# Batch 0's expert results from the result slots straight into the merge's buffer

## The reference

```
grouped = x.reshape(b, s // g, g, d)                       # groups of 32 tokens, 16 groups a batch
logits = einsum('bntd,des->bntes', grouped, Wc) + bc + tie
perm = (logits == max(logits, axis=-3))                    # every expert picks one token of each group
permuted = einsum('bntd,bntes->bnesd', grouped, perm)
inner = relu(einsum('bnesd,esdf->bnesf', permuted, W1) + b1)
result_permuted = einsum('bnesf,esdf->bnesd', inner, W2) + b2
result = einsum('bnesd,bntes->bntd', result_permuted, perm)
x = x + tanh(g_ffn[0]) * result
```

## Time and profile before

| | |
|---|---|
| median of 3 runs | 1321.31 us |
| lowest and highest | 1316.73 and 1325.94 us |
| profiled execution | 1322.05 us |
| its span, first to last instruction | 1320.3 us |
| mean granted TensorE clock | 0.986 |
| TensorE, VectorE, ScalarE, GpSimd busy | 1252.8, 887.4, 570.1, 552.6 us |
| DMA | 213.59 MB, mean 162 GB/s |

### The profile page before, as it was taken

One profiled execution on the slowest core, in us unless ns is written; L12 is line 12 of the kernel. 1 busy time (PEld: TensorE's weight loads), 2 busy tenths in 40 slices (PEclk: granted clock), 3 DMA queues, 4 the chain that ended last, 5 costly groups with the idle time before them and its releaser, 6 DMA issues.

```text
span 1320.3 us, 28354 instructions
## 1 busy us (share of the span) xinstructions
PE 1252.8 (95%) x10607; PEld 901.3 (68%) x10607; DVE 887.4 (67%) x1570; ACT 570.1 (43%) x1039; POOL 552.6 (42%) x456
## 2 busy tenths in 40 slices
PE   8999999999999978886999999999998999999998
PEld 7777677777777657621447666766775778887887
DVE  6985677777676455564547766766685977777762
ACT  4255245534442554453562443353336434333331
POOL 3303642553251100000339657866834644454540
PEclk9999999999999998998999999999998999999999
DMA  9885465234411678899993643563423111111100
GB/s 351 220 184 185 138 183 173 79 113 150 142 65 45 209 206 273 308 402 368 403 337 116 213 167 99 176 221 123 133 84 129 64 64 64 64 49 47 64 29 35
DMA packets 126502, 213.59 MB, mean 162 GB/s; under 512 B 27609, under 2 KB 49369, under 8 KB 122331
## 3 DMA queue, kind: packets, MB, share of 16 engines
q1 hardware_dynamic: 126427, 212.57, 48.7%
HBM read 129.92 MB, written 82.62 MB: 161 GB/s over the span
## 4 chain that ended last, share of the span: by engine, by line
PE 76%; DVE 9%; DMA 5%; SPq 3%; issue 3%; ACT 3%; POOL 1%; DVEq 0%; ACTq 0%; POOLq 0%
PE b L157 12%; PE b L158 11%; PE b L159 11%; PE b L1606 5%; PE b L1805 5%; PE b L1806 4%; PE b L1807 4%; PE b L1577 4%; PE b L1712 3%; PE b L1720 3%; PE b L2135 3%; PE b L2101 3%; PE b L1626 2%; PE b L2119 2%; SPq L709 2%
## 5 line engine op out<-in xcount | busy, mean ns | idle before, releaser
L1169 ACT ACTIVATE a_pr<-b 120x512 f32<-120x512 f32 x252 | 130.1, 604 | 89.3 <-PE b L1606 89.3
L1358 DVE TENSOR_REDUCE a_mx<-b 128x4 f32<-128x480 f32 x256 | 151.8, 649 | 14.6 <-PE b L1577 14.4
L1050 POOL TENSOR_TENSOR a_rp<-a_rp,a_b2s 128x512 f32<-128x512 f32 x96 | 120.4, 1291 | 26.6 <-DMA a_rp<-s_rp 26.6
L1089 POOL TENSOR_TENSOR a_atl<-a_pvs,a_ath 128x512 fp32r<-128x512 f32 x64 | 81.2, 1302 | 79.1 <-ACT a_ath L1213 79.1
L1805 PE MATMUL b<-a_woh,a_ath 128*128 128x512 f32 x256 | 104.9, 410 | 3.1 <-POOL a_atl L1089 3.1
L157 PE MATMUL b<-a_xth,a_wqh 128*128 128x512 f32 x256 | 104.2, 407 | 0.6 <-DVE a_xtl L1333 0.4
L1807 PE MATMUL b<-a_woh,a_atl 128*128 128x512 f32 x256 | 101.8, 398 | 0.0
L158 PE MATMUL b<-a_xtl,a_wqh 128*128 128x512 f32 x256 | 101.8, 398 | 0.0
L1806 PE MATMUL b<-a_wol,a_ath 128*128 128x512 f32 x256 | 101.8, 398 | 0.0
L159 PE MATMUL b<-a_xth,a_wql 128*128 128x512 f32 x256 | 101.7, 397 | 0.0
L1503 DVE SCALAR_TENSOR_TENSOR a_x<-b,a_gate,a_x 128x512 f32<-128x512 f32 (+1 forms) x64 | 47.7, 745 | 72.5 <-PE b L1807 72.5
(11 more groups left out here) (245 smaller groups left out, 3127.3 us busy)
## 6 DMA issues: line engine op xcount, KB each, us to landing
a_rp<-s_rp SPq DMA_DIRECT2D x128, 256.0 KB, 4.6
s_x<-a_x SPq DMA_DIRECT2D x16, 1024.0 KB, 4.3
s_rp<-e_chosen SPq DMA_DIRECT2D x16, 1024.0 KB, 8.0
s_rp<-e_xc SPq DMA_DIRECT2D x16, 1024.0 KB, 8.0
e_w<-in_w SPq DMA_DIRECT2D x56, 256.0 KB, 5.1
a_xr<-in_x_t SPq DMA_DIRECT2D x8, 1024.0 KB, 6.5
a_x<-in_x SPq DMA_DIRECT2D x8, 1024.0 KB, 10.5
s_xn<-a_xn SPq DMA_DIRECT2D x8, 1024.0 KB, 4.6
```

Source lines behind the costliest of these rows:

```text
L1050: pool.tensor_tensor(rp[:, t, a], rp[:, t, a], b2s[:, :], ALU.add).then_inc(rp_biased, 1)
L1169: act.activation(pr[:, h % RING, :], bank[k][0:S2, :], ACT.Exp, scale=SCALE)\
L1358: dve.tensor_reduce(mx[:, t, :, r], bank[k][:, 0:HJ * S2].rearrange("p (a s) -> p a s", a=HJ), AX.X, ALU.max).then_inc(free[k], 1)
```

## The change

For batch 0, the rows go from the slot in SBUF to the merge's buffer `rp` in SBUF at once, and not by way of DRAM. For every unit below 16 and each of its two halves c, four transfers (one for each expert) bring 16 slot partitions x 2 KB into the one partition of `rp` that belongs to the expert, 32 KB each, and one transfer stores the other 48 partitions of the half to DRAM. These are ten transfers a unit where there was one; units 16 to 31 are stored as before. All ten count on `out_st`, so the counts are worked out by `stored`. The sixteen loads of batch 0 and SyncE's wait ahead of them are gone, and TensorE waits for `half_written` itself before each of the four tiles of batch 0. So that an expert's 16 rows lie in the order of `rp`, (t a), the gathered tiles go to `gt` with a step of 4 in place of 4 side by side, and the loads of the other batches read (j t a). The buffer `rp` moves to the head of the memory of `gt` (its first 32 KB), `wqh` and `wql` behind it.

```diff
-        allot(early, "wqh wql xth xtl rp xn permb b2h b2l bo x qh ql pvs woh wol pr ath atl kbd kl mpick vals pick bc b2s mx "
+        allot(early, "rp wqh wql xth xtl xn permb b2h b2l bo x qh ql pvs woh wol pr ath atl kbd kl mpick vals pick bc b2s mx "
@@ load_experts
-        src = io["rp"][of].rearrange("u (c j a t) s d -> (u c) s j t a d", c=2, a=GT, t=NT)
+        src = io["rp"][of].rearrange("u (c j t a) s d -> (u c) s j t a d", c=2, a=GT, t=NT)
@@ load_behind
         if u == HALF_U:
-            front.half_written(sp)
-            for t in range(NT):
-                load_experts(sp, 0, t)
             load_query_weight(sp)
@@ add_experts_bias
-                pool.wait_ge(rp_in[t], 16 * GT * (j + 1))
+                pool.wait_ge(rp_in[t], 16 * GT * j)
@@ merge_tile
-                pe.wait_ge(rp_in[t], 16 * GT * (j + 1))
+                if i is None:
+                    front.half_written(pe)
+                else:
+                    pe.wait_ge(rp_in[t], 16 * GT * j)
@@ experts.sync
-            sp.dma_start(io["rp"][2 * u // EK][u % (EK // 2)], slot(u)).then_inc(out_st[u % RO], 16)
+            if u < EK // 2:
+                for c in range(2):
+                    at, own, e = c * NH, NG // B, 2 * EJ * u + EJ * c
+                    for j in range(EJ):
+                        sp.dma_start(behind[0].rp[e + j:e + j + 1].rearrange("s t a d -> s (t a) d"),
+                                     slot(u)[at:at + own, j, :]).then_inc(out_st[u % RO], 16)
+                    sp.dma_start(io["rp"][0][u][at + own:at + NH], slot(u)[at + own:at + NH]).then_inc(out_st[u % RO], 16)
+            else:
+                sp.dma_start(io["rp"][1][u - EK // 2], slot(u)).then_inc(out_st[u % RO], 16)
             behind[0].load(sp, u)
 
-    def half_written(sp):
+    def stored(n):
+
+        return 16 * (2 * (EJ + 1) * min(n, EK // 2 // RO) + max(n - EK // 2 // RO, 0))
+
+    def half_written(eng):
         for q in range(RO):
-            sp.wait_ge(out_st[q], 16 * (EK // 2 // RO))
+            eng.wait_ge(out_st[q], stored(EK // 2 // RO))
@@ gathered
-        ts = slice(TS * a, TS * (a + 1))
+        ts = slice(a, GS, 4)
@@ scalar and vector, results(p)
-                act.wait_ge(out_st[u % RO], 16 * (u // RO))
+                act.wait_ge(out_st[u % RO], stored(u // RO))
```

More of the change, by code:

```diff
@@ L86 @@
 Begun = namedtuple("Begun", "load_ahead gather emptied evict_act evict_dve on_act chosen")
-Behind = namedtuple("Behind", "load act dve pe")
+Behind = namedtuple("Behind", "load act dve pe rp")
 Front = namedtuple("Front", "cleared half_written written groups_read spare_banks banks")
@@ L1841, in attention @@
             Behind(load_behind, lambda act, k: scalar(act, k), lambda dve, k: vector(dve, k),
-                   lambda pe, k: tensor(pe, None, k))
+                   lambda pe, k: tensor(pe, None, k), rp)
     ahead = Ahead(load_weights, load_first, load_first_keys, load_second, load_output_weight, constants, first_norm, query_weights_high, query_weights_low,
@@ L1983, in sync @@
                     sp.wait_ge(g_free[b], n + 1)
-            sp.dma_start(io["rp"][2 * u // EK][u % (EK // 2)], slot(u)).then_inc(out_st[u % RO], 16)
+            if u < EK // 2:
[7 more added lines that the diff above has]
+                sp.dma_start(io["rp"][1][u - EK // 2], slot(u)).then_inc(out_st[u % RO], 16)
             behind[0].load(sp, u)
-    def half_written(sp):
+    def stored(n):
+        return 16 * (2 * (EJ + 1) * min(n, EK // 2 // RO) + max(n - EK // 2 // RO, 0))
+    def half_written(eng):
         for q in range(RO):
-            sp.wait_ge(out_st[q], 16 * (EK // 2 // RO))
+            eng.wait_ge(out_st[q], stored(EK // 2 // RO))
     def written(eng, q):
-        eng.wait_ge(out_st[q], 16 * (EK // RO))
+        eng.wait_ge(out_st[q], stored(EK // RO))
     def gathered(c, s, a):
         b, _ = use(SETS * c + s, a)
-        ts = slice(TS * a, TS * (a + 1))
+        ts = slice(a, GS, 4)
         dst = gt[:, :, s, :, ts] if turned(c) else gt[:, s, :, :, ts]
@@ L2050, in results @@
             if p % 2 == 0 and u >= RO:
-                dve.wait_ge(out_st[u % RO], 16 * (u // RO))
+                dve.wait_ge(out_st[u % RO], stored(u // RO))
             for q in range(2):
```

## The result

| | before | after |
|---|---|---|
| median (range) of 4 runs each | 1323.62 us (1316.73 to 1327.86) | 1432.76 us (1426.43 to 1435.18) |
| profiled execution, its span | 1322.05, 1320.3 us | 1426.43, 1424.6 us |
| granted clock, mean of the span | 0.986 | 0.948 |

The changed kernel takes 1.0808 times as long, 95% interval 1.0774 to 1.0842. The forecast was 1473 us with a range of 1345 to 1515: direction and range hold, the size is 40 us too large.

What follows compares the result with a forecast made beforehand. TensorE bounds most of the kernel, but the full DMA engines bound the expert results. Units 0 to 15 at 12.6 us with constants +158.6, unit 16's store +2.5, loads -10.0: +151 on 1322.05 gives 1473 us, range 1345 to 1515.

Steps and rivals of the forecast that it cites:

- Part 1: Expert results: batch 0's sixteen loads and the queue's wait ahead of them go, -10.0 us, at most 17.2.
- unit 16's store: Expert results: this store, ahead of the point where units 0 to 15 are done before, falls behind it: +2.5 us.
- Part 2: Expert results: a unit's eight 32 KB transfers into one partition go at one engine's 26.3 GB/s, 10.0 us a unit.
- The keys' ratio of 1.41: Last keys' load: 32-partition rows hold the engines 1.41 times as long per byte, taken as sign that narrow destinations are slow.
- Part 3: Expert results: a unit's two 48-row stores take 2.6 us, 1.9 at the low end; with the transfers 12.6 a unit.
- Part 4: SyncE's queue: ten issues a unit at 0.36 to 0.47 us, 3.6 to 4.7 us, hidden under 12.6 us of data.
- Rival C: Expert results: one partition takes the full rate and SyncE's issues bound: +12 us, 1334 us; chance 0.12.
- Part 5: Edits at nothing: TensorE's wait before the merge and the step-4 gathered evictions cost 0 us; evictions above 650 ns would refute it.
- The sum: Whole kernel: units 0 to 15 and constants +158.6, unit 16's store +2.5, loads -10.0, so +151 us to 1473 us.
- A: Expert results, main case: transfers and stores run serially, 12.6 us a unit: 1473 us, range 1432 to 1510; chance 0.68.
- B: Expert results: transfers into different partitions overlap; two at a time 7.6 us a unit, 1394 us, four 1353; chance 0.15.
- D: Expert results: direct transfers hide altogether, units keep 2.5 to 2.9 us: 1305 to 1312, say 1308 us; chance 0.05.

Runs made afterwards that it cites:

- e7: e1 without the two stores a unit, so the direct transfers alone (batches 1 to 3 load other data): 1375.14 us, a unit 6.5.
- e3: e1 with each direct transfer writing 2 KB into each of 16 partitions and not 32 KB into one: 1411.51 us, a unit 8.78.
- e12: e4 with each direct transfer into 16 partitions and not one: 1383.99 us.
- e6: e1 without the direct transfers, so the two 48-row stores a unit alone (batch 0's buffer filled by one 4 MB load): 1335.92 us.
- e2: The kernel before with only the step-4 evictions and the loads' order that goes with them: 1337.18 us, ratio 1.0078.
- e1: The changed kernel with gathered evictions writing four side by side again, rp in order (a t), and a later SyncE wait before loading x: 1416.93 us.
- e8: e4 and e5 together: one whole store and four direct transfers from SyncE, four from ScalarE: 1353.12 us, a unit 5.06.
- e10: e8 with each direct transfer into 16 partitions and not one: 1345.28 us, a unit 4.78.
- e5: e1 with the four direct transfers of the half c = 1 issued from ScalarE's queue, not SyncE's: 1378.17 us, a unit 6.65.
- e9: e7 (direct transfers alone) with each transfer into 16 partitions and not one: 1365.09 us, a unit 5.53.
- e11: e1 with a unit's eight direct transfers first and then both 48-row stores: 1411.48 us, a unit 8.91.
- e4: e1 with one whole store of 128 rows a unit in place of the two of 48: 1388.62 us, a unit 7.25.

## Why the prediction was right, and where it was not

**What bounds the kernel before**: read rightly. The units stood on the critical path; 101.7 us more for them became 104 us of the whole.

**Part 1** held: from the units' end to the kernel's end it is -10.7 us; the -10.0 of the loads and the +2.5 of unit 16's store make -7.5.

**Part 2** is the step that failed. It put the unit's pace at eight transfers of one partition, 10.0 us at one engine's 26.3 GB/s, with sixteen engines held behind it. The rate was not far off for such transfers alone (e7: 34 GB/s at first, some 56 later), but in the changed kernel all transfers together kept the engines at a share of 0.57, and a wider destination changes the kernel by next to nothing (e3, e12). The keys' ratio of 1.41 was a true sign of a real effect, which was then given the whole unit.

**Part 3**: 2.6 us for the two stores; e6 has 2.64 for them alone in its last eight units. The sum 10.0 + 2.6, one behind the other, fell with part 2.

**Part 4** is where the pace was. "Under 12.6 us of data this is hidden" hid what decides. The price was too low as well: 0.36 to 0.47 us an issue came from the shortest and the median ones in the earlier trace rows, issues that stand singly or in fours. A better row was at hand: the earlier trace rows has sixteen back to back in 10.66 us, 0.67 each, and with 16 x 10 x 0.67 us for the units C's sum is already 1382 us. Here they are 0.59 back to back, and the issue behind each store adds 1.2 us: 8.7 a unit and not 3.6 to 4.7. Rival C named the mechanism, the share "well below 1, SyncE's queue without gaps" word for word, and with these two prices its own sum, 558.84 + 16 x 8.7 + 4.4 + 2 = 704.4 us, is +99.3 for the units, +91.8 with part 1, 1414 us. With the evictions' 13.3 that is 1427, and the profiled execution took 1426.43; that is a sum after the fact, with prices from the result. I gave it 0.12.

**Part 5** was half wrong. TensorE's wait at the merge cost nothing that the trace shows. The evictions did: "above 650 ns would make part 5 wrong", and they are at 1133 and 1083. That is 13.3 us at the first result transfer, 10.7 in the whole kernel by itself (e2), some 18 by the ratios when undone, or 6.8 by the spans (e1): the sign is settled, the size between these. The 598 and 690 ns that I took for "free" compare a pattern of four side by side with straight rows; neither says anything about single floats.

**The sum.** Forecast +151, measured +104.4 in the profiled executions: the units -56.9 (148.0 and not 204.9), the evictions +13.3, the end -3.2. The forecast came near since a wrong mechanism had about the size of the right one, and since two errors had opposite signs: that the time fell into the range was luck. There is also a slip in it: stores twice as long add 16 x 2.6 = 41.6 us, so the upper end of A is 1515 and not 1510.

**Rivals.** B's overlap did not decide: the engines are not kept busy enough for it to matter. Some overlap there is, since e7's 34 and 56 GB/s are 1.3 and 2.1 times the 26.3 of one engine. D needed a unit of 3.4 us. No kernel with the rows in their places came below 5.06 (e8), and even with sixteen partitions and two queues it is 4.78 (e10), so none beats the kernel before.

## What to carry to other kernels

Count issues before bytes: a transfer of 32 KB took 0.63 us of the issuing queue, so one queue could bring no more than 52 GB/s of them, and the DMA share tells which it is (near 1: data; 0.57 with a queue that has no gaps: issues). Price an issue by rows in which many stand back to back, not by the shortest. When a change only reorders what an eviction writes, look at the step in bytes between neighbours: 16 bytes made it 1.9 times as long on ScalarE and 1.6 times on VectorE. And when work is moved to a second issuing queue, look at the chain again: in e5 the pace moved with it.

## What the runs showed of the hardware

- An eviction of 128x512 floats from PSUM that writes with a step of 16 bytes takes 1133 ns on ScalarE and 1083 on VectorE; with four floats side by side 598 and 687.
- Issues of transfers out of the slots take 0.58 to 0.59 us back to back on SyncE, for 32 KB, 384 KB or 1 MB alike, where nothing holds them; a single one 0.36. The small constants between them are at 0.43 (e9's queue, below), so it is not every issue that costs 0.59; what sets it is open.
- Among direct transfers, a store out of the slot makes one issue behind it 1.2 us longer (48 rows of 8 KB; e1, e3, e11) or 0.8 us (128 rows; e4, e12). Open why.
- The four issues on ScalarE's queue take 0.71 and 0.98 us in the median in e5, 0.63 and 0.64 in e8.
- Transfers of 32 KB into one partition after the other hold all sixteen engines at 34 GB/s, later at some 56 (e7); into sixteen partitions they move 52 GB/s at a share of 0.24 (e9).
- Two stores of 48 rows, each from one half of the partitions, move 298 GB/s alone (e6, last eight units), where the whole store moved 421.

```profile
608.35 0.43 SPq L724 DMA_DIRECT2D a_gate<-in_g_xattn  x1
```
